# Storing the routing weights of a mixture of experts element by element, without the transpose on TensorE

## What is computed

```python
router = xf @ Wg                                   # 8 experts
top_logits, idx = jax.lax.top_k(router, 2)
probs = jax.nn.softmax(top_logits)
w = zeros((n, 8)).at[arange(n)[:, None], idx].add(probs)
h = silu(einsum('tc,ech->eth', xf, W1)) * einsum('tc,ech->eth', xf, W2)
y = einsum('eth,ehc,te->tc', h, W3, w)             # w weighs the experts
y = y + (silu(xf @ Ws1) * (xf @ Ws2)) @ Ws3        # the shared expert
x = x + 0.5 * y
# the Mamba block: projection, causal convolution, and per channel and state
# h = dA_t * h + dBx_t over the tokens, y_t = sum over 16 states of h * C_t
```

## Time and profile before

| | |
|---|---|
| median of 3 runs | 1839.37 us (1837.52 to 1846.04) |
| the profiled execution | 1839.04 us, span 1837.3 us |
| busy: PE, DVE, ACT, POOL | 1658.7, 1478.3, 1266.2, 1445.7 us |
| busy share of the span: PE, DVE, ACT, POOL | 90%, 80%, 69%, 79% |
| granted PE clock, mean | 0.96 of full speed |
| transfers | 121287 packets, 304.54 MB, mean 166 GB/s |

### The profile page before, as it was taken

How to read it: one execution, slowest core, us unless ns; L and a number is a source line. 1 busy time by engine, 2 the same in 40 slices (tenths; PEclk the granted TensorE clock), 3 DMA queues, 4 the chain that set the end, 5 groups by cost and what they waited for, 6 DMA issues and landing times.

```text
span 1837.3 us, 24041 instructions
## 1 busy us (share of the span) xinstructions
PE 1658.7 (90%) x7378; PEld 1001.5 (55%) x7378; DVE 1478.3 (80%) x2241; ACT 1266.2 (69%) x2030; POOL 1445.7 (79%) x1366
## 2 busy tenths in 40 slices
PE   5898788999999999999999999999999999958488
PEld 3454445556555555656555555656555555534255
DVE  1438889989798988989798988989898998989732
ACT  2367678787877778776867777786877777665422
POOL 3336869888898988888888888888898888887753
PEclk9998889999999999999999999999999999969599
DMA  6026768687776868686777867777677868767642
GB/s 158 24 87 141 180 150 193 160 205 173 185 184 162 207 156 201 158 194 170 178 184 170 201 158 189 181 187 184 168 190 172 196 156 192 184 152 186 143 104 69
DMA packets 121287, 304.54 MB, mean 166 GB/s; under 512 B 19299, under 2 KB 40518, under 8 KB 106822
## 3 DMA queue, kind: packets, MB, share of 16 engines
q0 software_dynamic: 18432, 125.84, 34.4%
q1 hardware_dynamic: 98406, 174.46, 33.3%
q10 hardware_dynamic: 4320, 2.71, 0.5%
HBM read 167.67 MB, written 5.24 MB: 94 GB/s over the span
## 4 chain that ended last, share of the span: by engine, by line
POOL 43%; DMA 23%; issue 14%; PE 9%; DVE 7%; ACT 1%; SPq 1%; POOLq 0%; ACTq 0%; DVEq 0%
DMA yacc<-prod 19%; POOL prod L623 18%; POOL gated L555 14%; DVE hist L924 4%; DMA crow<-c_rows 3%; POOL yacc L619 2%; PE ps_y L1090 2%; DVE ps_db L876 2%; POOL yacc L640 1%; PE ps_h1a L1076 1%; SPq L418 1%; PE ps_h2a L1098 1%; PE ps_h1b L1076 1%; PE ps_h2b L1098 1%; POOL xres L610 1%
## 5 line engine op out<-in xcount | busy, mean ns | idle before, releaser
L623 POOL TENSOR_TENSOR prod<-hist,crow 128x1024 f32<-128x1024 f32 x224 | 556.5, 2484 | 204.7 <-DVE hist L924 171.0
L1090 PEld LDWEIGHTS ps_y<-down_w,gated 128*128 128x128 f32 (+1 forms) x3584 | 474.0, 196 | 276.4 <-issue 160.1
L924 DVE TENSOR_TENSOR_SCAN hist<-decay,ps_db 128x1024 f32<-128x1024 f32 x256 | 583.3, 2278 | 2.8
L555 POOL TENSOR_TENSOR gated<-gated,silu 128x512 f32<-128x512 f32 x352 | 493.3, 1450 | 74.4 <-DVE gated L904 71.4
L1090 PE MATMUL ps_y<-down_w,gated 128*128 128x128 f32 (+1 forms) x3584 | 491.8, 282 | 58.0 <-POOL gated L555 56.3
L876 DVE TENSOR_TENSOR ps_db<-du,ps_db 128x1024 f32<-128x1024 f32 x256 | 313.2, 1224 | 114.2 <-PE ps_db L1058 112.1
L686 ACT ACTIVATE decay<-delta,a_neg 128x510 f32<-128x510 f32 x512 | 326.8, 709 | 3.7 <-DVE delta L965 2.2
L706 ACT ACTIVATE silu<-ps_h1a 128x512 f32<-128x512 f32 (+1 forms) x224 | 132.9, 593 | 194.8 <-PE ps_h1a L1076 194.6
L1076 PE MATMUL ps_h1b<-xnT,up_w 128*128 128x512 f32 x448 | 236.7, 610 | 3.6 <-ACT silu L706 3.1
L1098 PE MATMUL ps_h2a<-xnT,up_w 128*128 128x512 f32 (+1 forms) x448 | 236.1, 609 | 1.9 <-DVE gated L904 1.9
L1076 PE MATMUL ps_h1a<-xnT,up_w 128*128 128x512 f32 (+1 forms) x448 | 236.4, 609 | 0.0
(11 more groups left out here) (136 smaller groups left out, 1937.5 us busy)
## 6 DMA issues: line engine op xcount, KB each, us to landing
yacc<-prod POOLq DMA_DIRECT2D x112, 1024.0 KB, 10.0
crow<-c_rows SPq DMA_DIRECT2D x128, 512.0 KB, 5.0
wrow<-w_rows SPq DMA_DIRECT2D x320, 128.0 KB, 6.3
wrow<-w_rows SPq DMA_DIRECT2D x64, 224.0 KB, 7.0
wrow<-w_rows SPq DMA_DIRECT2D x64, 192.0 KB, 6.4
wrow<-w_rows SPq DMA_DIRECT2D x64, 160.0 KB, 2.9
yacc<-yacc POOLq DMA_DIRECT2D x16, 512.0 KB, 7.8
wrow<-w_rows SPq DMA_DIRECT2D x64, 96.0 KB, 2.9
```

The costliest lines, as they stand in the source:

```text
L555: nc.gpsimd.tensor_tensor(gated[:, pos % NGATE, :], gated[:, pos % NGATE, :], silu[:, (pos + NCHUNK * f_parity(of, f)) % NSILU, :], ALU.mu ...
L623: nc.gpsimd.tensor_tensor(prod[:, (pair - 1 + odd) % 2, s % 2, :, :], hist[:, s % 2, :, :], c_all, ALU.mult).then_inc(prod_done, 1)
L924: nc.vector.tensor_tensor_scan(hist[:, s % 2, :, :].rearrange("p h t -> p (h t)"), decay[:, s % NA, :, :, :].rearrange("p h b t -> p (h b ...
L1090: ins = nc.tensor.matmul(ps_y[:, t * C:(t + 1) * C], gated[0:rd, posd % NGATE, t * P:(t + 1) * P], down_w[0:rd, jd, :], start=(posd == 0 a ...
```

## The change

The transposes `wT0` and `wT1` on PE and ACT's copy out of `ps_m` are dropped. `wtok` is laid out with experts outside and the four token tiles inside, and SP stores it in `w_rows` directly, each of the 128 x 32 values to its own place in the rows of DRAM. The half that was in the copy is multiplied once, at the start, into the up weights of the experts (`up_w[:, 1, 0:EH]`), and PE waits for that. POOL now waits for the store of the route before, before it writes `wtok` again; ACT's copy of C no longer waits for `w_stored`. Beside this the counting of steps, turns and waits is written in another way (tables over all iterations in place of formulas), with the same order of all other instructions. The core of the diff:

```diff
-        15: ["in3", "ln_scale"], 16: ["wT0", "ln_shift"], 17: ["dt0"], 18: ["dt1", "ln_add"], 19: ["stats1"],
+        15: ["in3", "ln_scale"], 16: ["ln_shift"], 17: ["dt0"], 18: ["dt1", "ln_add"], 19: ["stats1"],
...
-        25: ["rcopy1", "route1"], 26: ["cT", "delta"], 27: ["bT", "tilt1"], 28: ["weights1", "du"], 30: ["wT1"],
+        25: ["rcopy1", "route1"], 26: ["cT", "delta"], 27: ["bT", "tilt1"], 28: ["weights1", "du"],
...
-        wtok = sb("wtok", [P, TILES, E])
+        wtok = sb("wtok", [P, E, TILES])
...
             def store_w(k, f):
 
-                sp.wait_ge(misc_taken, turn(k, f"wT{f}"))
-                sp.dma_start(w_rows[f, :, :], wT).then_inc(w_stored, 16)
+                sp.wait_ge(wtok_ready, route_no(k, f"tilt{f}") + 1)
+                with nc.allow_non_contiguous_dma(reason="the routing weights are stored by experts"):
+                    sp.dma_start(w_rows[f, :, :].rearrange("e (t p) -> p (e t)", p=P),
+                                 wtok[:].rearrange("p e t -> p (e t)")).then_inc(w_stored, 16)
...
-                            nc.gpsimd.tensor_tensor(wtok[:], hotp[:, :, 0, :], hotp[:, :, 1, :], ALU.add
+                            if n > 0:
+                                pool.wait_ge(w_stored, 16 * n)
+                            nc.gpsimd.tensor_tensor(wtok[:].rearrange("p e t -> p t e"), hotp[:, :, 0, :], hotp[:, :, 1, :], ALU.add
                                                     ).then_inc(wtok_ready, 1)
...
+            act.wait_ge(experts_loaded, 16 * N_EXPERTS)
+            nc.scalar.activation(up_w[:, 1, 0:EH], up_w[:, 1, 0:EH], ACT.Copy, scale=0.5).then_inc(up_halved, 1)
...
-                        elif step == "wT0" and enters(k) or step == "wT1" and tail(k):
-                            take(k, step)
-                            if not isinstance(k, int) or route_no(k, step) > 0:
-                                act.wait_ge(w_stored, 16 * route_no(k, step))
-                            held = k + 2 if step == "wT1" and lead(k) else k + 1
-                            if not isinstance(k, int) or 0 < held <= G:
-                                act.wait_ge(c_stored, 16 * held)
-                            nc.scalar.activation(wT, ps_m[0:E, :], ACT.Copy, scale=0.5).then_inc(misc_taken, 1)
-                        elif step == "cT" and lead(k):
-                            take(k, step)
-                            act.wait_ge(w_stored, 16 * (route_no(k, "wT0") + 1 if enters(k) else route_no(k, "wT1")))
+                        elif step == "cT":
+                            take(it, step)
+                            if it >= 0:
+                                act.wait_ge(c_stored, 16 * (it + 1))
                             nc.scalar.activation(cT[:], ps_m[0:NS, :], ACT.Copy).then_inc(misc_taken, 1)
...
             pe.wait_ge(experts_loaded, 16 * N_EXPERTS)
+            pe.wait_ge(up_halved, 1)
...
-                        elif step == "wT0" and enters(k) or step == "wT1" and tail(k):
-                            pe.wait_ge(wtok_ready, route_no(k, step) + 1)
-                            claim(k, step)
-                            to_rows(wtok, E, ident, ps_m).then_inc(misc_full, 1)
```

More of the change, by code:

```diff
@@ L91, in macaron_kernel @@
     }
[L93 to L100, removed]
     SETUP_MADE, SETUP_TAPS, SETUP_EDGE = 16, 24, 28
-    def first(k):
-        return isinstance(k, int) and k == -2
+    PLANS = {k: START_PLAN for k in range(-2, FULL)}
+    UNITS = {k: START_UNIT for k in range(-2, FULL)}
+    SP_PLANS = {k: START_SP for k in range(-2, FULL)}
     def enters(k):
-        return not isinstance(k, int) or 0 <= k + 2 < G
+        return 0 <= k + 2 < G
@@ L110, in lead @@
     def lead(k):
[L111 removed]
+        return 0 <= k + 1 < G
     def scans(k):
[L114 removed]
+        return 0 <= k < G
     def tail(k):
[L117 removed]
+        return 0 <= k - 1 < G
     def last(k):
[L120 to L168, removed]
-        n = ECHUNK * (2 * odd + 1 - f) + e
-        return n % NW, 2 * 16 * (2 * ECHUNK // NW) * (k - odd) + 2 * 16 * (n // NW + 1) + (
-            2 * 16 * (2 * ECHUNK % NW) // NW) * (k - odd)
@@ L173, in unit @@
-    def unit(k, odd, slot, lag):
-        back = slot < lag
-        of, parity = (k - 1, 1 - odd) if back else (k, odd)
-        units = START_UNIT if start(of) else UNIT
-        if slot - lag + back * SLOTS not in units:
-            return None
-        f, pos = units[slot - lag + back * SLOTS]
-        return (of, parity, f, pos) if (last(of) if f else enters(of)) else None
-    def home(engine, group):
-        return group % XS if isinstance(group, int) else engine.snap(group % XS)
-    def iterations(engine, body):
+        return 0 <= k - 2 < G
@@ new lines, in macaron_kernel @@
+    ALL = [(name, it) for k in range(-2, G + 2) for slot in range(SLOTS) for name, it in steps(k, slot)]
+    MISC = {step: n + 1 for n, step in enumerate(s for s in ALL if s[0] in MISC_NAMES)}
+    ROUTES = [(it, name[4]) for name, it in ALL if name in ("tilt0", "tilt1")]
+    STAT_STEPS = [s for s in ALL if s[0] in ("stats0", "stats1", "stats2", "stats3")]
+    UNIT_AT = {}
+    for k in range(-2, G + 2):
+        for slot, (f, pos, *shift) in UNITS.get(k, UNIT).items():
+            it = k + sum(shift)
+            if (last(it) if f else enters(it)):
+                UNIT_AT[(k + 2) * SLOTS + slot] = (it, f, pos)
@@ L189, in iterations, with unit, home @@
+    def unit(k, slot, lag):
+        return UNIT_AT.get((k + 2) * SLOTS + slot - lag)
+    def home(group):
+        return group % XS
+    def iterations(body):
         for k in range(-2, G + 2):
@@ L546, in body @@
             def body(k, odd):
-                nxt = 1 - odd
-                behind = home(pool, k - 1) if tail(k) else 0
                 for slot in range(SLOTS):
-                    u = unit(k, odd, slot, JOIN)
-                    if u is not None and ORDER[u[3]] < ECHUNK:
-                        of, _, f, pos = u
+                    u = unit(k, slot, JOIN)
+                    if u is not None and ORDER[u[2]] < ECHUNK:
+                        of, f, pos = u
                         pool.wait_ge(h2_taken, fcount(of, f, NCHUNK, pos + 1))
@@ L883, in body @@
                 nonlocal fin_chain
-                nxt = 1 - odd
-                entering, ahead = home(dve, k + 2), home(dve, k + 1)
-                behind, oldest = home(dve, k - 1) if tail(k) else 0, home(dve, k - 2) if last(k) else 0
                 for slot in range(SLOTS):
-                    u = unit(k, odd, slot, GATE)
+                    u = unit(k, slot, GATE)
                     if u is not None:
-                        of, parity, f, pos = u
+                        of, f, pos = u
                         j = ORDER[pos]
```

450 lines of the change are left out of this document (242 added, 208 removed).

## The result

The changed kernel takes 2163.96 us (median of 4 runs, 2156.98 to 2172.79) against 1841.34 for the kernel before (median of 4 runs, three of them those of its table): a ratio of 1.176, with an interval of 1.173 to 1.179. The forecast was 1858 us, with a range up to 1930. The loss is seventeen times the one that was forecast, and far outside the range.

What follows compares the result with a forecast made beforehand. The prediction took POOL's products and their accumulating transfers as the bound, with SP's blocking list behind them. Start +3, late store at f=0 +20, f=1 0 and freed PE time -4 gave +19 on 1839, so 1858 us (range 1826 to 1930).

Steps and rivals of the forecast that it cites:

- the price of one element: In the new store of the weights: 13 ns for each 4-byte element, 3.3 us of packets per store (2.3 to 11).
- The wait for the accumulation: At f=0: most of the store's elements wait until POOL's accumulating transfer lands at 786.9, making a store of 12.3 us.
- no cost: At f=1, SP's second store: issued earlier, with POOL's queue quiet, its eight loads end at 731.1 as before; 0 us.
- the shares at which lateness was counted: At f=0, 0.7 of 2.0 us late in 14 iterations, +20 us; at f=1 with dear elements, half of 14 iterations.
- cancel: At the program's two ends: a longer exposed store is offset by PE no longer waiting for the route; 0 us.
- the two places and their slack: In SP's list: the stores at f=0 and f=1; at f=0 2.4 us of slack, used up at a 10.4 us store.
- the start: Before PE's first transpose: halving the up weights on ACT delays it from 18.39 to about 21.4; +3 us.
- the worth of PE's and ACT's freed time: Transposes and copies removed on PE and ACT: a fifth of at most 19 us comes back, -4 us.
- The third sign named at the end: Accumulating transfers beside the new store: they might become longer, which would make the forecast wrong; not counted, no size given.
- Faster: Rival: elements pass between the accumulation's packets, the store stays inside SP's slack, PE's time comes back; 1828 us, chance 0.25.
- hidden anyway: Rival: the store is in time, but PE's freed time is worth nothing; +3 us, 1842 us, chance 0.20.
- Dear writes: Rival: 4-byte writes to DRAM cost 43 ns or more each; +144 us, 1983 us, chance 0.10.

Runs made afterwards that it cites:

- 128-piece run: The changed kernel with the store of the weights in 128 pieces of 128 bytes in place of 4096 single elements: 1838.62 us, ratio 0.999.

## Why the prediction was wrong

*The step that failed* is the price of one element, "I take 13 ns: near the lower end", with 43 ns above it. Alone, an element costs an engine 45 ns and the store 4 us more, 15.6 us in all, where 3.3 + 1 were taken; for the 1 no row was given. Two rows misled. The earlier trace rows show packets that read small pieces, and such a transfer is as cheap as they say (4.2 us by elements). And a packet's time in the trace is not the time until it is written: here too the packets are 14 ns long, and the store is counted as landed 8 us after the last of them. The prediction named the gap ("the trace has no such write"), and then let the nearest small number stand in for it., the other end, came within 2 ns of the marginal price, which may be chance, since they show reads as well.

*The wait for the accumulation* is a second step that failed, with the opposite sign. 8.0 of the forecast's 12.3 us at f=0 were the wait until the accumulation had landed. In the runs about half of the elements pass before most of it (DMA view of 926 to 930 us), and the store of f=0 is 17.7 us in the mean of the middle where it is 15.65 alone: 2 us more, not 8. Its company is no peculiarity of f=0 either: at f=1, where the queue was called quiet, it is 19.0. Every kind of store tried is 2 to 5 us longer in the loop than the first one of the same kernel, at both places. The 12.3 us are nearer to the truth than the parts they were added from.

*What followed.* At f=0 the store is 18.0 us in the iteration shown, not 12.3. At f=1 the forecast was "no cost"; the store is 20.4 us there, and passes the slack of 7.2 by more than the one at f=0 passes its 10.4.

*The next error* is the shares at which lateness was counted: 0.7 at f=0, and a half in the rival's account of f=1. The table shows about the whole of it: with the lengths right, the forecast's shares give 0.7 x 7.3 x 14 + 0.5 x 11.8 x 14 = 154 us, full shares 267. Measured are 19.7 in each of 11 iterations, which makes 276 if the other three of the 14 lose as much.

*The last* is that the two ends of the program "cancel". The span grew by 333.8 us; 216 of it lie in the 11 iterations of the middle, 117 outside. If 276 belong to the 14 iterations, some 58 are left for the ends, 3 of these at the start. There each store stands bare: SP waits 15.65 us at the first.

*Right* were the mechanism (SP's list blocks, and the loads of the weights for DVE are what is late), the two places and their slack, the start (+2.8 us at PE's first transpose, +3 forecast), the worth of PE's and ACT's freed time (4, within the 6 +- 5 measured), the number of packets, and their recorded length at the first store (14 ns; between 984 and 990 us it is 40, from 166.9% of 96 us over 4050 packets). The third sign named at the end, that the accumulations themselves might become longer, did come: 15.2 and 16.5 us for those beside the two stores shown, where the median is 10.4.

*The rivals.* "Faster" and "hidden anyway" needed a store of at most 10.4 us, which is not met; the 128-piece run shows that even a cheap store would have given no gain clear of noise, so "faster" was not to be had by this change. Its mechanism, elements that pass between the packets of the accumulation, is nearer to the trace than the forecast's wait. "Dear writes" was the true case, in part by luck: its 20 us at f=0 are near the 18.0 because 8 us of a wait that is not there stand in for a store that is dearer even than its price. Its +144 us were too small by the shares, by the ends, and by the 7 us of lateness at f=1, where 12 were measured. It had 0.10, because nothing in the trace spoke for it, though nothing spoke against it either.

*The rule of the Trainium skill* (DMA: Bandwidth & Descriptors, "Rules for kernel authors"), that a last dimension that is not contiguous should be rearranged, was right here: 1.176 with single elements, 0.999 with pieces of 128 bytes. The price per packet of its section "Bandwidth", read for the whole transfer (43 us as an estimate), was too high by a factor near three: 15.6 us. The trace's 742 packets in a microsecond did refute the price, but not the rule; I let the one argument dispose of both.

*Left open:* why writes that lie closer than 64 bytes are dearer, how much of an iteration's 19.7 us the packets add by holding up the accumulations, and how much of a store's length in the loop is due to the accumulation and how much to the loads beside it. Also, whether the lower granted clock of PE (0.902 in the mean, 0.96 before), which comes with its longer idle times, adds to the loss: the iteration is 0.6 us longer than the slack account says.

## What to carry to other kernels

A transfer that a queue blocks on has a length of its own, apart from its packets: measure it from the issue to the first instruction that its wait releases, and for a shape that the trace doesn't hold, put that one transfer at the end of the kernel and look, before a price from another shape goes into a sum. Writing single elements to DRAM is the dear form (15.6 us for 16 KB, against 1.4 in pieces of 128 bytes and 4.2 for single elements read or kept on chip), so do a transpose where it is free, here on a PE whose freed time was worth some 6 us of 1839. Work out a queue's slack, and count what lies beyond it in full, for every time that the queue passes the place: here that came within 1.4 us of the iteration for waits up to 19 us.

## What the runs showed of the hardware

- Single 4-byte writes to DRAM cost by their neighbourhood: 4096 of them take 15.8 us with 16 in each 64 bytes, 10.9 with 4, 8.0 with 1, and hardly less beyond that (8.3 with one in 128 bytes, 7.1 with one in 512).
- Of the first store of the changed kernel, 15.65 us long, the last 8 us hold no recorded packet. Later, beside other transfers, the DMA view of 984 to 990 us shows SP's queue with more than all engines' time, which says that records overlap, and POOL's queue with ten packets:

```profile
q1 hardware_dynamic: 4050, 0.07, 166.9%
q0 software_dynamic: 10, 0.08, 40.5%
```

- An accumulation issued into this took 16.5 us to landing, where the median of the kernel is 10.4; POOL stands 5.29 us for it. So a store of single elements does hold up another queue's transfer. Holding SP up without these packets costs as much, so this is not needed for such a loss, but its share in it is open.
